# One V product moved from GpSimd to VectorE in a gathered cross-attention

## The reference

```python
Q, K, V = heads(query, Wq), heads(key, Wk), heads(value, Wv)
# flatK, flatV: rows of all levels of a binary tree over the 512 keys
nk = flatK[:, :, idx_table]            # 12 gathered rows for each query position
nv = flatV[:, :, idx_table]
self_logits = jnp.einsum('bhnd,bhnd->bhn', Q, K) * scale
nbr_logits = jnp.einsum('bhld,bhlnd->bhln', Q, nk) * scale
w = jax.nn.softmax(concat([self_logits[..., None], nbr_logits]), axis=-1)
out = jnp.einsum('bhln,bhlnd->bhld', w, concat([V[:, :, :, None, :], nv]))
x = _layernorm(x + out @ Wo.T + bo)
```

## Time and profile before

| | |
|---|---|
| Time of the profiled execution | 2283.89 us |
| Span of its records | 2282.0 us |
| PE (TensorE) busy | 1983.7 us, 87% |
| DVE (VectorE) busy | 1854.0 us, 81% |
| ACT (ScalarE) busy | 1057.0 us, 46% |
| POOL (GpSimd) busy | 1126.6 us, 49% |
| Gathers, L1690 | 384 of 967 ns on POOL, 201.35 MB |
| V products on POOL, L1718 | 96 of 1915 ns |
| Adds on DVE, L1500 | 384 of 698 ns |
| Mean granted TensorE clock | 0.95 |

### The profile page before, as it was taken

The page is one execution under the profiler, slowest core; times in us unless marked ns, Lnnn a source line. Parts: engine busy times, 40 slices in busy tenths (PEclk is TensorE's granted clock), DMA queues, the critical chain, the costliest instruction groups (busy, mean ns, idle before and its releaser), DMA issues.

```text
span 2282.0 us, 34451 instructions
## 1 busy us (share of the span) xinstructions
PE 1983.7 (87%) x11744; PEld 1042.1 (46%) x11744; DVE 1854.0 (81%) x2416; ACT 1057.0 (46%) x1854; POOL 1126.6 (49%) x1132
## 2 busy tenths in 40 slices
PE   5599999899999999876259998999999999989997
PEld 2244444344443444322125555555555555555555
DVE  7579888889898898877688888888888888888940
ACT  3255555455555555545114444444444444444443
POOL 3325555445364556363545645555546546456520
PEclk9799999999999999988569999999999999999999
DMA  5334343444444444434856657567567566576520
GB/s 181 115 119 137 121 140 113 153 130 150 138 130 148 129 129 139 128 124 172 273 188 234 220 188 256 194 208 257 181 232 245 198 222 234 194 246 221 198 75 19
DMA packets 188809, 392.51 MB, mean 172 GB/s; under 512 B 20692, under 2 KB 82260, under 8 KB 188632
## 3 DMA queue, kind: packets, MB, share of 16 engines
q1 hardware_dynamic: 133336, 188.91, 25.8%
q0 software_dynamic: 55296, 201.35, 25.4%
HBM read 312.33 MB, written 77.59 MB: 171 GB/s over the span
## 4 chain that ended last, share of the span: by engine, by line
DVE 25%; PE 9%; DMA 6%; POOL 5%; issue 5%; ACT 1%; DVEq 0%; POOLq 0%; ACTq 0%
DVE e_ps L1500 7%; DMA inputs<-kv_flat,idx_rows 6%; DVE swapped L1447 5%; DVE inputs L1496 5%; DVE inputs L1438 4%; POOL inputs L1690 3%; PE aux L899 3%; POOL inputs L1718 2%; PE o_ps L923 2%; PE misc_ps L923 1%; PE e_ps L859 1%; PE rows_ps L859 1%; DVE e_ps L1506 1%; DVE total L1477 1%; DVE swapped L1451 1%
## 5 line engine op out<-in xcount | busy, mean ns | idle before, releaser
L1690 POOL DMA_INDIRECT inputs<-kv_flat,idx_rows x384 | 371.5, 967 | 136.6 <-issue 93.7
L1374 DVE TENSOR_REDUCE neg_max<-rows_ps 128x1 f32<-128x512 f32 x512 | 326.5, 679 | 88.3 <-PE rows_ps L783 82.7
L728 PE MATMUL aux<-inputs 128*128 128x512 f16 x1536 | 356.9, 385 | 32.8 <-POOL inputs L1601 21.8
L899 PE MATMUL aux<-probs,queries 128*128 128x256 f16 x2048 | 356.2, 276 | 0.7 <-issue 0.7
L1500 DVE TENSOR_TENSOR e_ps<-e_ps,inputs 128x512 f32<-128x512 f32 x384 | 268.2, 698 | 42.6 <-POOL inputs L1718 20.9
L1101 ACT ACTIVATE probs<-e_ps 128x1024 f32<-128x1024 f32 x256 | 261.8, 1023 | 76.1 <-PE e_ps L815 75.5
L1718 POOL TENSOR_TENSOR inputs<-inputs,split_up 128x1024 f32<-128x1024 f32 x96 | 182.6, 1915 | 211.5 <-DVE split_up L1484 210.8
L899 PE MATMUL aux<-probs,keys 128*128 128x256 f16 x1024 | 281.8, 275 | 0.0
L728 PEld LDWEIGHTS aux<-inputs 128*128 128x128 f16 x1536 | 150.6, 99 | 218.0 <-POOL inputs L1601 21.8
L1415 DVE TENSOR_TENSOR probs<-probs 128x2048 f32<-128x2048 f32 x96 | 229.2, 2387 | 19.3 <-ACT probs L1101 19.2
L1447 DVE TENSOR_REDUCE swapped<-inputs 128x32 f32<-128x1024 f32 x192 | 229.8, 1211 | 0.0
(11 more groups left out here) (164 smaller groups left out, 3437.0 us busy)
## 6 DMA issues: line engine op xcount, KB each, us to landing
kv_flat<-nodes SPq DMA_DIRECT2D x128, 256.0 KB
nodes<-kv_flat SPq DMA_DIRECT2D x32, 512.0 KB
queries<-qk_dram SPq DMA_DIRECT2D x96, 128.0 KB, 2.7
keys<-qk_dram SPq DMA_DIRECT2D x96, 128.0 KB, 3.0
split_up<-in_pieces SPq DMA_DIRECT2D x40, 256.0 KB
inputs<-in_xT SPq DMA_DIRECT2D x8, 1024.0 KB, 6.3
inputs<-in_ctxT SPq DMA_DIRECT2D x8, 1024.0 KB, 7.5
qk_dram<-high SPq DMA_DIRECT2D x32, 256.0 KB, 2.2
```

The lines of the kernel that those rows point to most:

```text
L728: mm = pe.matmul(o[:], w_part[:, w, c, f], x_part[:, which, c, :], start=c + k == 0, stop=c == KC - 1 and k == 2)
L899: mm = pe.matmul(HB[c % 2][:, 0:RW], w[:, k, c * P:(c + 1) * P], x_part[:, k, half * RW:(half + 1) * RW], start=k + i == 0, stop=k == KC - ...
L1374: dve.tensor_reduce(neg_max[:, g % 2, at + i:at + i + 1], rows_ps[:, i, :], AX.X, ALU.max, negate=True).then_inc(max_done, 1)
L1690: pool.indirect_dma_start(nb[:, slot(lt, g), k, :], None, rows, bass.IndirectOffsetOnAxis(idx_rows[:, lt, at:at + 1], 0))\
```

## The change

`POOL_V_GROUPS` becomes (4, 5). VectorE makes the V product of group 3 too, between the two adds of group 2. GpSimd makes the products of groups 4 and 5 one after the other, both ahead of the gathers, and then issues its twelve gathers without a product between them. The semaphore counts follow from the two tuples. In the first tile of all, which has its own code (`cross_late`), the three products become two.

```diff
-POOL_V_GROUPS = (3, 4, 5)
+POOL_V_GROUPS = (4, 5)
 DVE_V_GROUPS = tuple(g for g in range(NG) if g not in POOL_V_GROUPS)
...
                     for lt in tiles(half_)[begun:]:
-                        weight_values(b, lt, POOL_V_GROUPS[:-1])
+                        weight_values(b, lt, POOL_V_GROUPS)
                         if more and lt >= TT - 2:
                             next_rows(b, *((0, 1, 0) if lt == TT - 2 else (1, TT, 1)))
-                        for k, i in enumerate(range((lt + 1) * NG + AHEAD, (lt + 2) * NG + AHEAD)):
+                        for i in range((lt + 1) * NG + AHEAD, (lt + 2) * NG + AHEAD):
                             if more or i < TT * NG:
                                 gather(b, i)
-                            if k == 1:
-                                weight_values(b, lt, POOL_V_GROUPS[-1:])
```

## The result

| | median of 4 runs | range |
|---|---|---|
| before | 2286.37 us | 2282.79 to 2293.26 |
| changed | 2455.35 us | 2451.12 to 2464.32 |

The ratio is 1.0724, 95% interval [1.0689, 1.0759]. The changed kernel's profiled execution has a span of 2462.5 us and a mean granted TensorE clock of 0.92. The forecast was 2281 us, and its range ended at 2298 us.

The account below looks back on a forecast made before the run. No engine was the bound; a chain of waits through GpSimd, VectorE, TensorE and gathers was. 6.5 + 1.0 - 1.2 - 7.5 - 1.0 - 4.4 = -6.6 us on 2287.67 us gave 2281 us, range 2262 to 2298 us.

Parts of the forecast that it names:

- the step on the gathers: Second tiles: without GpSimd's third product eight later DMAs issue 2.1 us earlier; bounds 0 and 2.1 us, 0.5 us taken.
- Product on VectorE: Product between two adds makes the last add 0.64 us (lt 0) or 0.29 us (lt 2) later; +6.5 us.
- my terms without the gathers and the clock: First tiles' later turns +6.5 us, very last tile +1.0 us, one long wait for GpSimd gone -1.2 us.
- Second tiles: Second of each two alternating tiles: earlier gathers shorten each by 0.5 us, 15 x -0.5 = -7.5 us.
- Clock: TensorE before first tiles' turns: less idle (3.66 to about 2.9 us) lifts clock 0.66 to 0.83 in four, -4.4 us.
- The sum: All terms over the 32 cross-attention tiles: 6.5 + 1.0 - 1.2 - 7.5 - 1.0 - 4.4 = -6.6 us.
- Rival A: DMA queue is full anyway, so earlier gather issues gain nothing: +4.1 us, 2292 us; chance 0.20.
- Rival B: TensorE's clock stays up in about 13 first tiles, 1.15 us each: -15 us, 2266 us; chance 0.25.
- Rival C: VectorE becomes the bound, its added 0.98 us hidden in neither tile: +17 us, 2305 us; chance 0.12.
- what I listed as signs of error: Second tiles keeping their length, granted clock rising to 1.00, or new waits for L1500 in the middle of the gathers.

Follow-up runs that it names:

- e8: Kernel before plus an idle GpSimd multiply of 1.9 us behind the eighth gather, so no run of issues exceeds four; 2304.68 us, ratio 1.0033.
- e1: Changed kernel with group 5's V product back behind the first four gathers, VectorE keeping four products; 2301.17 us, ratio 1.0025, chip 7.
- c5: Repeat on chip 11 of the changed kernel with group 5's V product back behind the first four gathers; 2299.97 us, ratio 1.0034.
- e9: Changed kernel plus an idle GpSimd multiply of 1.05 us behind the fourth gather; 2291.51 us, ratio 0.9973, chip 9.
- c2: Kernel before, unchanged, run again on chip 1; 2292.08 us, ratio 0.9999.
- c7: Repeat of e9 (changed kernel, idle multiply of 1.05 us behind the fourth gather) on chip 6; 2295.21 us, ratio 0.9992.
- e11: Changed kernel plus an idle GpSimd multiply of 0.62 us behind the fourth gather; 2293.91 us, ratio 0.9987, chip 6.
- c8: Repeat of e11 (changed kernel, idle multiply of 0.62 us behind the fourth gather) on chip 4; 2290.13 us, ratio 0.9976.
- e10: Changed kernel plus an idle GpSimd multiply of 1.05 us behind the sixth gather; 2295.88 us, ratio 1.0002, chip 6.
- e2: Kernel before with GpSimd's products of groups 3, 4 and 5 all ahead of the twelve gathers; 2304.04 us, ratio 1.0040, chip 7.

## Why the prediction was wrong

- **Failed: the step on the gathers.** I took GpSimd's third product as a delay that "holds the eight later DMAs", and bounded its removal from 0 to a gain of 2.1 us per tile. On some chips it was also the break that kept TensorE's updates at most 2.6 us late. Removed, they come up to 11 us late, 6.1 us per tile or 166 us in all. The lower bound should have gone below nothing: none of my rows shows twelve issues in a run. The trace of before had the signs, in the waits behind the runs of eight (`L1167 <- remote`) and in its one run of twelve, with an update 3.6 us late. The first of these cost nothing that a run here could win back (e8), but both show that a run of issues can make an update late.
- **Product on VectorE, right.** From GpSimd's first product the last add ends after 13.87 us in the changed kernel (1809.69 + 5.30 - 1801.12), in first and second tiles alike. In first tiles before, the mean was 13.43 us with lt 0 and 13.56 with lt 2, and so the turn came 0.44 and 0.30 us later in the kernels with a short break. Predicted: 0.64 and 0.29. e1 and c5, which have this part and not the earlier gathers, cost 2294.47 x 0.0025 = 5.7 us and 2291.68 x 0.0034 = 7.8 us; my terms without the gathers and the clock are 6.5 + 1.0 - 1.2 = 6.3 us. Both intervals reach from about 1 to 14 us, so this agrees but proves little.
- **Second tiles, near in size but not shown.** With the break of 0.6 or 1.05 us they take 33.4 to 33.6 us (lt 1) and 34.3 to 34.8 (lt 3), against 34.0 to 34.3 and 34.4 to 34.9 in the two profiles of before. The mean is some 0.4 us less, where I had 0.5, where the fifth gather is issued 0.8 us earlier behind S than before (e9, 11.5 against 12.3 us; without the idle product it is 1.7 us earlier, not the 2.1 I had); but the two profiles of before differ by 0.3 to 0.5 us among themselves. The direction is borne out by VectorE's waits for rows, 56.7 to 62.8 us in the five profiles with a break of 0.6 or 1.05 us, against 80.3 and 83.7 before.
- **Clock, wrong.** Without lateness TensorE's idle before a first tile's turn did not shrink: in e9 it is 4.2 us with lt 0 (2.9 before) and 3.4 with lt 2 (3.3 before), and the granted clock over the 10 us around the turn went from 0.83 to 0.76 and from 0.75 to 0.80. The second profile of before (c2) has 0.83 and 0.84, so for lt 2 there is no change clear of the spread, and for lt 0 the clock got worse. So the -4.4 us were not there. Why the idle grew with lt 0 is not shown.
- **The sum.** It said -6.6 us. With a short break it is 2296.16 x 0.0027 = 6.2 us less (e9), 1.8 (c7), 3.0 (e11) and 5.5 (c8), and 0.5 us more with the break behind the sixth gather (e10): 3.2 us less on average. What the sum describes is the changed kernel without late updates. There it is about twice too good, and without the clock's term it would have said -2.2 us.
- **Rival A, out as far as the rows tell:** 407 GB/s in place of 305 where A had the queue full, and the shorter waits for rows above. The Trainium skill (DMA: Bandwidth & Descriptors, section Where 436 GB/s comes from) puts the HBM side at about 358 GB/s per core. In the stretch in question before had 305 GB/s, which such a bound allows, and the changed kernel 407, which it does not, so the measurement decides against it.
- **Rival B, out:** the mean clock fell from 0.95 to 0.92 as TensorE stood idle 7 us at a time, and in the kernels without lateness it is 0.94 to 0.95.
- **Rival C, the only one on the side that came about, had the wrong mechanism.** GpSimd's waits for L1500 at the gathers are 42.0 us in the changed kernel, against 39.0 before. In e1 and c5 they grew to 95.6 and 91.6 us, but the issues don't come later for it, and these kernels are only 0.3% slower. Nothing in what I listed as signs of error would have named the late updates, but the time and the chain of waits did at once.

The Trainium skill (GPSIMD Engine Reference, section Engine selection) advises VectorE for elementwise work on a tile, since GpSimd is about two times slower with two inputs. The rows agree in kind, 1.91 us against 1.21 us for the same product, 1.58 times. Followed here it made the kernel 7% slower on the chips with lateness, since what GpSimd did beside it mattered more than who was quicker.

## What to carry to other kernels

Before you take work out from between DMA issues on GpSimd, ask what the pause did for others: a dense run of twelve indirect DMA issues held TensorE's semaphore updates for up to 11 us on three of six chips, and a break of 1 us behind the fourth was enough to bring that down to 3 us, which cost nothing. In a program on one core, suspect behind every wait that the profile puts down to "remote" an update that came late: compare the time of the update with the end of the instruction that raises it, and look for a run of issues ahead of it. Repeat a surprise on a second chip before explaining it, since e2 on chip 7 alone would have buried the right theory.

## What was not expected of the hardware

- Late updates are TensorE's alone. In the tile shown the first of them belongs to L906, 4.9 us after the first gather's issue (1806.14 to 1811.08), and the three held longest come together 2.4 us after the last issue ended (1820.93 to 1823.35).
- They differ from chip to chip (each seen on one occasion): chips 1, 9 and 11 have them, chips 4, 6 and 7 none over 0.1 us, with the same kernel 7% apart (e2: 2304.04 and 2474.60 us), while the kernel before takes 2291 to 2297 us on all of them.
- They hardly depend on the bytes: up to 9.7 us late with rows of 2 KB and up to 11.0 us with rows of 4 KB.
- They need more than the run of issues: in the changed kernel's second tile of all, with an unbroken run of twelve, two updates 8.7 and 11.3 us behind the first issue were on time.
- Open: what in the chip holds the updates, what else it takes, whether the issues or the time for which the DMA engines are occupied bring it about, why some chips don't do it, and where between 0.20 and 1.05 us the break becomes long enough. The changed kernel itself never came to a chip without lateness. That it would be within about 0.5% of before there is an estimate, from e2 (ratio 1.0040), which has its unbroken run, and from the kernels with a short break (0.9976 to 1.0002).
